# GNN kernel: the one-hots of the low key are made on GpSimd, and the ring of one-hots has 16 places

## The reference

```
edge_index = stack([src, dst])
h = relu(layernorm(x));  x = x + L0(h, edge_index)                 # softmax attention over edges
h = relu(layernorm(x));  x = x + L1(h, src, dst)                   # segment_sum of h[src] into dst
h = relu(layernorm(x));  x = x + L2(h, edge_attr, src, dst)        # two MLPs per edge, segment_sum
h = relu(layernorm(x));  x = x + L3(h, src, dst, edge_type)        # 4 steps: segment_sum by type, GRU cell
```

## Time and profile before

| what | us |
|---|---|
| median of three runs | 14872.25 |
| lowest and highest run | 14870.82, 14874.32 |
| the profiled execution, span from the first to the last instruction | 14882.7 |
| building stage in it, from 327.4 to 3466.4 | 3139.0 |
| busy in the whole span: PE | 11422.5 |
| busy in the whole span: DVE | 6097.0 |
| busy in the whole span: ACT | 3555.1 |
| busy in the whole span: POOL | 4598.0 |

### The profile page before, as it was taken

The page is one execution under the profiler, slowest core; times in us unless marked ns, Lnnn a source line. Parts: engine busy times, 40 slices in busy tenths (PEclk is TensorE's granted clock), DMA queues, the critical chain, the costliest instruction groups (busy, mean ns, idle before and its releaser), DMA issues.

```text
span 14882.7 us, 281691 instructions
## 1 busy us (share of the span) xinstructions
PE 11422.5 (77%) x60408; PEld 6477.4 (44%) x60409; DVE 6097.0 (41%) x28511; ACT 3555.1 (24%) x9549; POOL 4598.0 (31%) x4343
## 2 busy tenths in 40 slices
PE   2666655667999777667777766776689999999999
PEld 2333333333223355555555555555554444444443
DVE  6888888885554333333333333333320000000000
ACT  0444444443222022222222222222210000000000
POOL 2000000000000078888888888888500000000000
PEclk7666666667999889999999999999779999999999
DMA  2333333332211633333333333333559989899898
GB/s 93 104 104 104 101 102 103 104 101 91 79 74 65 257 37 41 42 41 41 42 41 42 41 42 41 41 41 41 40 196 342 341 330 341 330 341 342 330 341 303
DMA packets 1120447, 2096.58 MB, mean 141 GB/s; under 512 B 372941, under 2 KB 982880, under 8 KB 1012496
## 3 DMA queue, kind: packets, MB, share of 16 engines
q1 hardware_dynamic: 823736, 1913.57, 36.6%
q0 software_dynamic: 295904, 174.34, 11.5%
HBM read 1630.27 MB, written 457.23 MB: 140 GB/s over the span
## 4 chain that ended last, share of the span: by engine, by line
PE 49%; issue 22%; POOL 15%; DVE 8%; DMA 1%; DVEq 1%; SPq 1%; ACT 1%; POOLq 0%; another core or an unknown queue 0%; ACTq 0%
PE ps L1467 15%; POOL G L490 8%; PE ps L1472 8%; PE ps L1129 8%; POOL reverse L813 6%; PE ps L1184 4%; DVE hots L1795 2%; PE ps L1175 2%; DVE hots L1794 2%; DVE hots L1793 2%; PE ps L1187 1%; PE ps L1409 1%; DMA reverse<-SD,sidx 1%; POOL scatter_hold L812 1%; PE ps L1270 1%
## 5 line engine op out<-in xcount | busy, mean ns | idle before, releaser
L1129 PE MATMUL ps<-hots 128*128 128x392 f16 x4859 | 1882.1, 460 | 1247.6 <-issue 766.8
L813 POOL DMA_INDIRECT reverse<-SD,sidx x1660 | 2653.4, 1598 | 390.1 <-issue 379.8
L1467 PE MATMUL ps<-chunk,feat 128*128 128x512 f16 (+1 forms) x10192 | 2279.5, 375 | 14.4 <-DVE feat L2141 13.4
L843 ACT ACTIVATE stagebuf<-ps 128x392 f32 x3248 | 1477.3, 502 | 1690.0 <-PE ps L1132 1599.0
L490 POOL DMA_INDIRECT G<-h_table,idx x1660 | 1653.1, 996 | 493.6 <-issue 486.9
L1995 DVE TENSOR_TENSOR acc<-acc,ps 128x132 f32 x1660 | 484.7, 292 | 3125.6 <-PE ps L1333 3050.7
L1330 PE MATMUL ps<-MS,OH 128*128 128x128 f32 x3320 | 781.9, 319 | 1261.3 <-issue 782.3
L1467 PEld LDWEIGHTS ps<-chunk,feat 128*128 128x128 bf16 x10192 | 943.1, 98 | 1342.9 <-issue 349.5
L1793 DVE TENSOR_SCALAR hots<-count_lo,key_lo 128x128 f16<-128x128 f16 x4859 | 1193.8, 246 | 568.5 <-PE ps L1132 567.5
L1795 DVE TENSOR_SCALAR hots<-count_hi,key_hi 128x294 f16<-128x294 f16 x4859 | 1410.2, 290 | 0.0
L920 ACT ACTIVATE SD<-ps 128x129 f32<-128x129 f32 x1660 | 461.9, 278 | 3815.6 <-DMA reverse<-SD,sidx 3803.6
(11 more groups left out here) (415 smaller groups left out, 15563.6 us busy)
## 6 DMA issues: line engine op xcount, KB each, us to landing
chunk<-adj SPq DMA_DIRECT2D x720, 1792.0 KB, 8.9
adj<-stagebuf SPq DMA_DIRECT2D x406, 784.0 KB, 5.3
chunkA<-adj SPq DMA_DIRECT2D x48, 1792.0 KB, 6.7
chunk<-adj SPq DMA_DIRECT2D x60, 1232.0 KB, 7.4
G<-in_edge SPq DMA_DIRECT2D x1660, 32.0 KB
G<-h_table,idx POOLq DMA_INDIRECT x1660
reverse<-SD,sidx POOLq DMA_INDIRECT x1660
reverse<-acc SPq DMA_DIRECT2D x4, 3225.0 KB, 20.0
```

What stands on the lines that cost most here:

```text
L813: nc.gpsimd.indirect_dma_start(reverse[j % R], bass.IndirectOffsetOnAxis(sidx[:, j:j + 1], 0), SD[:, j % R, :], None, compute_op=ALU.add). ...
L843: nc.scalar.activation(stagebuf[:, bass.ds(held["word"][j] >> ENDBITS, SLEN)].rearrange("p (x c) -> p x c", c=BLK)[:, :, 0:2], bank[j % 8] ...
L1129: nc.tensor.matmul(ps[:, bass.ds(held["banks"][j % STEPW] & 7 * 512, 2 * COMBS)], hots[:, j % BRING, 0:P], hots[:, j % BRING, P:P + 2 * CO ...
L1467: nc.tensor.matmul(bank[k % 2][:, 0:cols], feat[0][:, hi, 0:2, :].rearrange("p a d -> p (a d)"), columns(chunk4, i % DRING, m, cols), star ...
```

## The change

In the building stage, the compare with `key_lo` leaves VectorE. GpSimd makes it, four steps at a time: it copies four columns of `key_lo` to one of two slots of the new tile `lowslot`, waits for that copy by the new semaphore `low_made`, and makes four compares with the slot's columns; the last of them increments `low_made` again, so a batch counts three. TensorE waits at each batch for `low_made` as well as for `hot_made`. GpSimd's former loop and `room_made` are gone: ScalarE loads the counts of stores itself and waits for `events_done`. The ring of one-hots has 16 places; GpSimd waits for room in it once in four steps, VectorE at each step as before, and their loops are 16 steps long.

```diff
--- before.py
+++ after.py
@@ -75,7 +75,7 @@
 NGRP = 13
 NREG = BW * 2 // BLK
 NEV = NREG + OV * 2 // BLK
-BRING = 8
+BRING = 16
 STEPW, VIRTW, BATCH = 16, 16, 4
 ENDBITS = 13
 SWEEP = 64
@@ -249,6 +249,7 @@
         stagebuf = here("stagebuf", [P, (SBUFS + OBUFS) * SLEN + BLK], F16)
         hots = here("hots", [P, BRING, P + 2 * COMBS], F16)
         zero16 = here("zero16", [P, P], BF16)
+        lowslot = here("lowslot", [P, 2, BATCH])
         hots_f = stagebuf[:, 0:2 * BPAD].bitcast(F32)
         phase.close()
         inner.close()
@@ -378,8 +379,8 @@
             sem(n) for n in ("tab_cols", "tab_turned", "tab_copied", "tab_stored", "tab_loaded"))
         step_known, key_gathered = sem("step_known"), [sem(f"key_gathered{h}") for h in range(2)]
         key_masked, key_turned, key_copied = sem("key_masked"), sem("key_turned"), sem("key_copied")
-        hot_made, step_done, room_made, evicted, events_done = (
-            sem(n) for n in ("hot_made", "step_done", "room_made", "evicted", "events_done"))
+        hot_made, low_made, step_done, evicted, events_done = (
+            sem(n) for n in ("hot_made", "low_made", "step_done", "evicted", "events_done"))
         stored = [sem(f"stored{q}") for q in range(2)]
         word_made = sem("word_made")
         built = sem("built")
@@ -775,21 +776,23 @@
 
             pool.wait_ge(tab_loaded, 16 * 10)
 
-            def words(row, k, top):
-                _, v = nc.values_load_multi_w_load_instructions(
-                    virttab[row:row + 1, k:k + VIRTW] if known(k) else virttab[row:row + 1, bass.ds(k, VIRTW)], engines=(pool.engine,),
-                    min_val=1, max_val=top,
-                    skip_runtime_bounds_check_because="the path's tables are made of counts within these bounds")
-                return v
-
-            held = {}
-
-            def mark(k, j, it):
-                if j == 0:
-                    held["ring"] = words(64, k, NEV + EPRE)
-                pool.wait_ge(events_done, held["ring"][j] & 255)
-                pool.sem_inc(room_made, 1)
-            pipeline(pool, VW, VIRTW, 0, lambda it, j: stage(VW, VIRTW, it, j, 0, mark))
+            pool.wait_ge(hot_made, 1)
+
+            def low(k, j, it):
+                if j % BATCH:
+                    return
+                if not (known(k) and k < BRING):
+                    pool.wait_ge(step_done, k + (BATCH - BRING))
+                n = min(BATCH, BSTEPS - k) if known(k) else BATCH
+                slot = lowslot[:, j // BATCH % 2, 0:n]
+                nc.gpsimd.tensor_copy(slot, part(key_lo[:, :], k, 1, 0, n)).then_inc(low_made, 1)
+                pool.wait_ge(low_made, k // BATCH * 3 + 1 if known(k) else it * (BRING // BATCH * 3) + j // BATCH * 3 + 1)
+                pool.sem_inc(low_made, 1)
+                for m in range(n):
+                    last = nc.gpsimd.tensor_scalar(hots[:, j + m, 0:P], count_lo[:, :], lowslot[:, j // BATCH % 2, m:m + 1], None,
+                                                   ALU.is_equal)
+                last.then_inc(low_made, 1)
+            pipeline(pool, BSTEPS, BRING, 0, lambda it, j: stage(BSTEPS, BRING, it, j, 0, low))
 
 
             pool.wait_ge(table_stored, 16)
@@ -832,13 +835,21 @@
 
             held = {}
 
+            def room(k):
+                _, v = nc.values_load_multi_w_load_instructions(
+                    virttab[64:65, k:k + VIRTW] if known(k) else virttab[64:65, bass.ds(k, VIRTW)], engines=(act.engine,),
+                    min_val=1, max_val=NEV + EPRE,
+                    skip_runtime_bounds_check_because="the path's tables are made of counts within these bounds")
+                return v
+
             def evict(k, j, it):
                 if j == 0:
                     _, held["word"] = nc.values_load_multi_w_load_instructions(
                         virttab[96:97, k:k + VIRTW] if known(k) else virttab[96:97, bass.ds(k, VIRTW)], engines=(act.engine,),
                         min_val=1, max_val=((SBUFS + OBUFS - 1) * SLEN + BLK - 1 << ENDBITS) - 1,
                         skip_runtime_bounds_check_because="the path's tables are made of counts within these bounds")
-                act.wait_ge(room_made, k + 1)
+                    held["room"] = room(k)
+                act.wait_ge(events_done, held["room"][j] & 255)
                 act.wait_ge(step_done, held["word"][j] & ((1 << ENDBITS) - 1))
                 nc.scalar.activation(
                     stagebuf[:, bass.ds(held["word"][j] >> ENDBITS, SLEN)].rearrange("p (x c) -> p x c", c=BLK)[:, :, 0:2],
@@ -1125,6 +1136,7 @@
                     held["banks"] = words(32, k, STEPW, 1, 7 * 512 * 4097)
                 if j % BATCH == 0:
                     pe.wait_ge(hot_made, min(k + BATCH, BSTEPS) if known(k) else k + BATCH)
+                    pe.wait_ge(low_made, k // BATCH * 3 + 3 if known(k) else it * (SWEEP // BATCH * 3) + j // BATCH * 3 + 3)
                     pe.wait_ge(evicted, held["free"][j // BATCH] & 4095)
                 nc.tensor.matmul(ps[:, bass.ds(held["banks"][j % STEPW] & 7 * 512, 2 * COMBS)], hots[:, j % BRING, 0:P],
                                  hots[:, j % BRING, P:P + 2 * COMBS],
@@ -1790,7 +1802,6 @@
             def hots_of(k, j, it):
                 if not (known(k) and k < BRING):
                     v.wait_ge(step_done, k - BRING + 1)
-                nc.vector.tensor_scalar(hots[:, j, 0:P], count_lo[:, :], part(key_lo[:, :], k, 1), None, ALU.is_equal)
                 nc.vector.tensor_scalar(hots[:, j, P:P + 2 * NB], count_hi[:, 0:2 * NB], part(key_u, k, 1), None, ALU.is_equal)
                 nc.vector.tensor_scalar(hots[:, j, P + 2 * NB:P + 2 * COMBS], count_hi[:, 2 * NB:2 * COMBS],
                                         part(key_hi[:, :], k, 1), None, ALU.is_equal).then_inc(hot_made, 1)
```

## The result

The changed kernel takes 15250.2 us (15246.7 to 15251.2 in three runs) against 14872.3 us: the ratio is 1.0254, with a 95% interval from 1.0236 to 1.0272. It is slower by 378 us. The forecast was 14907, in a range that ended at 15190. What came has the look of the second rival, GpSimd as the bound, with a loss near the upper end of the +50 to +400 that it was given. It has two causes, though: turns with VectorE, which the rival named, and a price of the compare above the bound that the prediction had set for it. That both together stay inside the rival's size is luck.

What follows compares the result with a forecast made beforehand. The prediction took TensorE's instruction stream as the building stage's bound. Its terms -96 + 114 - 5 + 22 + 0 gave +35 us on 14872.3, so 14907 us, with a range of 14855 to 15190.

Steps and rivals of the forecast that it cites:

- the second rival: Building stage: GpSimd and VectorE take turns at SBUF and the pair becomes the bound; mostly +50 to +400 us, chance 0.33.
- What bounds the kernel before: Building stage: TensorE's instruction stream sets the pace; waits for VectorE beyond ordinary boundaries and table loads are about 96 us.
- What it removes: Building stage: VectorE's shorter step and the ring of 16 together take away TensorE's waits, -96 us at most.
- What it adds on TensorE: One more register instruction at each of 1199 batch heads, 0.095 us each: +114 us, less 5 for overlap.
- What it adds on ScalarE: 203 more table loads, 1.1 us longer holes between evictions, a tenth of it on the path: +22 us.
- What it adds on GpSimd: Key copy, wait and four compares a batch: 0.38 us a step, between 0.33 and 0.54, hidden under TensorE's pace.
- The two engines together: Mutual exclusion of GpSimd and VectorE in the building stage: GpSimd's step 0.48 us, VectorE's 0.56 at most, so 0 us.
- a cover of 0.27 us a step: GpSimd's room in the building stage between its predicted 0.38 us a step and TensorE's 0.651.
- rival 2: Same as the second rival; serialised at start-to-start times, 0.36 + 0.34 = 0.70 us a step, +262 us; chance 0.33.
- the signs foretold for rival 2: L1805 and L1806 over 245 and 290 ns or further apart, GpSimd's compare well over 0.3 us, TensorE waiting at most batches.
- The chance of 0.33: The chance given to GpSimd and VectorE taking turns at SBUF and becoming the building stage's bound.

Runs made afterwards that it cites:

- The ring alone: The kernel before with the ring of one-hots at 16 places instead of 8, nothing else changed: 14789.3 us against 14876.3, ratio 0.9942.
- the rest of the change: The changed kernel without GpSimd's compares: ring of 16, ScalarE counts places, TensorE's third wait, VectorE makes all three compares: 14935.0 us against 14882.5 for the kernel before.
- the fastest kernel: The kernel before with a ring of 16 and TensorE waiting for VectorE once in 8 steps instead of 4: 14744.8 us against 14876.3, ratio 0.9912.

## Why the prediction was wrong, point by point

**What bounds the kernel before.** Right: TensorE's instruction stream, with about 96 us of waits for VectorE. The ring alone took 87 of them. The price of a register instruction at a boundary, 0.095 us, was 0.10. It stands in the trace 1184 times, not 1199, which is 1 us.

**What it removes.** The -96 was right in size, but it belongs to the ring alone. The prediction gave it to "these together" and didn't ask what each of the two is worth. VectorE at 0.52 us a step was under the 0.646 of the stage all along, by the prediction's own numbers, so moving a compare away from it could give nothing that a longer lead would not give.

**What it adds on TensorE.** +114 forecast (109 in the sum, with 5 taken off for overlap), +120 measured with the ring of 16: nothing overlapped. (With the ring of 8 it would have been +45.)

**What it adds on ScalarE.** +22 forecast, +19 measured; the added load takes 1.9 us and not 1.0, and the sum came out right all the same.

**What it adds on GpSimd: the step that failed.** "No row shows this compare. The nearest are the selects over 128x128", and from there 0.38 us a step, with 0.54 as the upper bound. Measured without VectorE's compares beside it, 2.68 us a batch in the median and 2.72 in the mean, 0.67 to 0.68 a step: above that bound, because the compares follow each other at 0.58 us where the bound had 0.45. The copy and the wait for it were priced right (0.35 forecast, 0.36 measured). Since TensorE alone would have needed 0.656 (its 3189 us in 4859 steps), the price alone made GpSimd the bound. The mechanism had been priced beforehand ("each 0.01 us a step over 0.651 costs 49 us"). Counted from the 0.656 that was measured, a mean of 0.679 gives about 112 us by that rule, and 107 were measured (3296 against 3189).

**The two engines together: failed too.** The prediction took 0 and wrote that it decides everything. That reasoning let the turns vanish under a cover of 0.27 us a step, and with a compare of 0.6 us there is no cover. They cost 3519 - 3296 = 223 us, 0.046 a step, less than the 0.10 that the prediction allowed for them. (Of the 649 ns in the mean, the 46 over 603 are the same 223 us in 4859 compares.) So the size was on the safe side; it was the cover that was missing. Serialisation at start-to-start times, as rival 2 had it, isn't what happens: 0.36 of VectorE and 0.67 of GpSimd would be over 1 us a step, and it is 0.72.

**Summed up:** the rest of the change +53 (forecast +35), GpSimd's own price about +107, turns about +223: 383, where 378 were measured. Of the signs foretold for rival 2, GpSimd's compare well over 0.3 us came. TensorE waits for it at about half of the batch heads (571 of 1214), not at most. L1805 and L1806 are longer than before, by 13 and 32 ns, but this sign proves little: with all of the change but GpSimd's compares, and so nothing of GpSimd's beside them, the same two lines are already at 260 and 306 ns in the mean.

```profile
L1789 DVE TENSOR_SCALAR hots<-count_hi,key_hi 128x294 f16<-128x294 f16 x4857 | 1487.4, 306 | 0.0
L1788 DVE TENSOR_SCALAR hots<-count_hi,early 128x98 f16<-128x98 f16 x4856 | 1263.1, 260 | 0.0
```

The chance of 0.33 and the bounds on the compare's price were what was wrong. A price without a row had been bounded by a different instruction times 1.5 to 2; the instruction turned out at 2.4 times the select's pace from start to start (0.580 against 0.245).

The Trainium skill ("SBUF — State Buffer", Who interferes with whom) has it that a VectorE instruction in a two-port mode and a GpSimd instruction exclude each other, for a whole instruction. The runs agree that the two get in each other's way (600 ns alone, 723 in the mean beside three compares of VectorE). For how long they do at a meeting, and whether these compares of VectorE run in such a mode, no run here settles: many compares of GpSimd that run beside VectorE's stay at 600 ns, and the 1018 longest take 0.18 us more. The Trainium skill ("GPSIMD Engine Reference", 4.1 Engine selection) calls one-input work on GpSimd roughly line-rate. This doesn't agree with the runs: the price per column is 2.5 ns here and 274 ns stand beside it, for an operation of one input that VectorE does in 246 ns in all, at 45 / 196 = 0.23 ns a column. The measurement decides.

## What to carry to other kernels

Before work is moved off a producer that is late, compare its mean pace with the consumer's: if it is faster on average, it needs a longer lead and no relief, and the ring alone gives the gain (here -87 us for one number). A wait that is put on the engine whose instruction stream is the bound costs its instruction each time (0.10 us here), and a test of it on a kernel that has other waits shows too little (+45 instead of +120). An instruction that no row shows is to be bounded by what the plan can bear, not by the nearest other instruction: here the plan breaks, by this working, at 0.565 us a compare from start to start (four steps of 0.656 less the 0.36 that a batch has beside its compares, 2.68 - 4 x 0.58), and that was the number to have doubts about.

The same working points at a variant that no run tested. At 0.58 us the compare misses that number by little, and what lifts GpSimd over TensorE's pace is as much the copy of the keys and the wait for it, 0.36 us a batch. An estimate from these numbers: a form of the compare that needs no copy would take GpSimd 0.58 + 0.05 for the turns = 0.63 us a step, just under TensorE's 0.656. TensorE would be the bound again, near the +53 of the rest of the change and still behind the -87 of the ring alone.

## What the runs showed of the hardware

- GpSimd's TENSOR_SCALAR with is_equal over 128 partitions: 592 ns at the least with 128 columns, 433 with 64; 600 to 603 with no compare of VectorE beside it, and 0.58 us from start to start. An f32 input changes nothing. A constant instead of a per-partition scalar shortens the duration to 527 ns and leaves the smallest distance between starts at 0.589.
- GpSimd's compare and VectorE's one-input f16 compares slow each other, and GpSimd loses more: beside three of VectorE's a step it takes 723 ns in the mean instead of 600, and loses 0.13 us a step; VectorE's three take 0.555 us from start to start instead of 0.525.
- TensorE's granted clock over its steps was 0.69 in the fastest kernel, 0.67 with the ring alone, 0.63 before, 0.55 with the rest of the change and 0.52 in the changed kernel (its levels are 1.2 and 2.4 GHz), so a mean between the two levels each time. The steps inside a batch stayed 0.37 us apart in all of them.
- TensorE's table loads took from 1.10 us up to 7.3, and the long ones go with the stores: of the 304 loads of 16 banks in the kernel before (up to 3.9 us), the 181 during which the store queue had no packet in flight took 1.10 us on average, and the 107 with more than ten in flight in the mean 2.89. The 7.3 belongs to the other 76, which load 16 eviction counts. No run changed the stores, so that they are the cause isn't shown.
